# A transformer stack on one NeuronCore: register loops over the batches against a program that is written out

## The reference

```python
# L0
qh, kh, vh = q @ w_q, k @ w_k, v @ w_v            # 16 heads of 64
attn = einsum('bhqd,bhkd->bhqk', qh / sqrt(64), kh) + add_attn
attn = softmax(where(mask == 0, -1e9, attn))
out = layernorm(einsum('bhqk,bhkd->bhqd', attn, vh) @ w_o + residual)
# L1, twice: x with itself (masked), x with ctx_1024 (not masked), 16 heads of 32
x = layernorm(x + mha(x, memory))
# feed-forward
x = layernorm(x + relu(x @ w1 + b1) @ w2 + b2)
```

## Time and profile before

| | us |
|---|---|
| median of 3 runs | 4304.11 (4303.60 to 4305.34) |
| the profiled execution, as timed | 4310.14 |
| its span in the trace | 4308.4 |
| PE busy | 4168.9 (97%) |
| DVE busy | 3336.0 (77%) |
| ACT busy | 2840.6 (66%) |
| POOL busy | 1618.3 (38%) |

### The profile page before, as it was taken

How to read it: one execution, slowest core, us unless ns; L and a number is a source line. 1 busy time by engine, 2 the same in 40 slices (tenths; PEclk the granted TensorE clock), 3 DMA queues, 4 the chain that set the end, 5 groups by cost and what they waited for, 6 DMA issues and landing times. The chain is left out here.

```text
span 4308.4 us, 79964 instructions
## 1 busy us (share of the span) xinstructions
PE 4168.9 (97%) x23152; PEld 3401.2 (79%) x23152; DVE 3336.0 (77%) x6955; ACT 2840.6 (66%) x6169; POOL 1618.3 (38%) x1801
## 2 busy tenths in 40 slices
PE   7999999999999999999999999999999999999999
PEld 6888888888888777777777777777777767888887
DVE  6777778788888889889988999998899995333334
ACT  6666666666666678888888889888888883111111
POOL 2222222232333345555555546556555651110101
PEclk9999999999999999999999999999999999999999
DMA  2221112112111210000000021100101111100100
GB/s 94 66 64 51 61 51 81 49 62 69 51 61 51 77 59 21 26 31 30 31 15 31 23 72 47 40 25 32 35 30 37 54 57 64 40 29 34 49 29 35
DMA packets 108998, 200.82 MB, mean 47 GB/s; under 512 B 12208, under 2 KB 12208, under 8 KB 108720
## 3 DMA queue, kind: packets, MB, share of 16 engines
q1 hardware_dynamic: 108720, 197.73, 14.0%
HBM read 155.73 MB, written 41.94 MB: 46 GB/s over the span
## 5 line engine op out<-in xcount | busy, mean ns | idle before, releaser
L1672 POOL TENSOR_SCALAR QS<-QK 32x1024 fp32r<-32x1024 f32 (+2 forms) x1152 | 1164.8, 1011 | 1448.1 <-DVE QK L1351 626.5
L1174 ACT ACTIVATE R<-psT 128x512 fp32r<-128x512 f32 x1536 | 913.1, 594 | 453.8 <-PE psT L926 439.8
L1166 ACT ACTIVATE PR<-PR,MN 128x512 f32<-128x512 f32 x1536 | 1103.0, 718 | 56.0 <-DVE MN L1336 37.8
L1444 DVE TENSOR_TENSOR R<-psT,R 128x512 fp32r<-128x512 f32 x1536 | 1046.7, 682 | 27.2 <-issue 14.1
L926 PE MATMUL psT<-ID,PR 128*128 128x128 f32 x6144 | 928.6, 274 | 31.4 <-DVE R L1444 24.5
L926 PEld LDWEIGHTS psT<-ID,PR 128*128 128x128 f32 x6144 | 754.2, 141 | 258.6 <-issue 26.6
L1336 DVE CUSTOM_DVE_ANT_0 PR<-psS,RAW 128x512 f32<-128x512 f32 x1024 | 699.0, 683 | 284.0 <-PE psS L907 231.8
L948 PE MATMUL psV<-R 128*64 128x512 f32 (+1 forms) x3072 | 895.6, 400 | 11.7 <-DVE OG L1364 10.4
L948 PEld LDWEIGHTS psV<-R 128*64 128x64 f32 (+1 forms) x3072 | 457.0, 154 | 176.9 <-DVE R L1444 12.6
L910 PE MATMUL psS<-QS 128*128 128x512 f32 x1024 | 466.1, 455 | 28.1 <-DVE MN L1336 9.8
L1196 ACT ACTIVATE PR<-psS,COLS 128x512 f32<-128x512 f32 x128 | 88.3, 690 | 549.1 <-PE psS L866 549.1
(11 more groups left out here) (128 smaller groups left out, 8248.7 us busy)
## 6 DMA issues: line engine op xcount, KB each, us to landing
x<-Y SPq DMA_DIRECT2D x96, 256.0 KB, 2.1
RAW<-x SPq DMA_DIRECT2D x96, 256.0 KB, 2.7
Y<-x SPq DMA_DIRECT2D x96, 256.0 KB, 3.5
RAW<-in_ctx_t SPq DMA_DIRECT2D x92, 256.0 KB, 2.8
RAW<-in_w SPq DMA_DIRECT2D x68, 256.0 KB, 2.8
RAW<-in_x SPq DMA_DIRECT2D x60, 256.0 KB, 3.6
RAW<-in_side SPq DMA_DIRECT2D x60, 256.0 KB, 2.5
Y<-in_x SPq DMA_DIRECT2D x32, 256.0 KB, 4.2
```

What stands on the lines that cost most here:

```text
L1166: nc.scalar.activation(prob(st, k), prob(st, k), ACT.Exp, bias=MN[:, k % 8:k % 8 + 1], scale=-1.0, accum_out=row_sums(st, SM, g)[:, qt, j: ...
L1174: nc.scalar.activation(PT[h % 2][:, 0, :, qt * P:(qt + 1) * P], turned(place[st.name][k]).rearrange("p (k t) -> p k t", k=NT), ACT.Copy).t ...
L1444: nc.vector.tensor_tensor(lo, turned(place[st.name][k]).rearrange("p (k t) -> p k t", k=NT), f32(hi), ALU.subtract).then_inc(t_evac, 1)
L1672: nc.gpsimd.tensor_scalar(to, pair, 1.0, 1.0, ALU.mult, ALU.mult).then_inc(stacked, 1)
```

## The change

The five register loops are gone. `passes` and the programs of FF now call the middle batch six times in a Python loop, so each batch of each stage has its own instructions, every wait compares with a constant, and no engine branches. `turns`, `counts`, the lists of names and the three `gate` functions with all their calls are taken out; what a wait needs is now carried by the instruction itself or by a waiting instruction ahead of it. The computing instructions and their order on every engine are the same. The program of PE grows from 10,088 to 25,949 instructions, that of DVE from 3,521 to 7,055, of ACT from 2,527 to 5,073, of POOL from 1,615 to 2,448, of SP from 780 to 843.

```diff
@@ Tally @@
     def done(self, n):
-        v = self.unit * (n + 1) + self.credit
-        return v if self.turn is None else self.turn * (self.per * self.unit) + v
+        return self.unit * (n + 1) + self.credit
...
-@contextmanager
-def turns(eng, count, tallies):
-
-    first = [t.n for t, _ in tallies]
-    with eng.Fori(0, count) as r:
-        for t, per in tallies:
-            t.per, t.turn = per, r
-        yield r
...
@@ passes @@
-                with turns(eng, B - 2, [(tal[k], per[k]) for k in dict.fromkeys(own) if k in tal]) as r:
-                    run(middle_pass(i), r + 1)
+                for batch in range(1, B - 1):
+                    run(middle_pass(i), batch)
                 run(last_pass(i), B - 1)
...
@@ SP, the load of x @@
                 sp.wait_ge(x_hi, tal["x_hi"].done(n - 2))
-                gate()
                 sp.dma_start(xs[:, tal["xs"].slot(i)], dram[src][b, tt * P:(tt + 1) * P, :]).then_inc(
                     tal["xs"].sem_of(i), 16)
...
@@ PE, FF @@
-            with turns(pe, B - 2, [(tal["xs"], NT), (tal["j"], NT), (tal["u"], NF), (tal["h"], NF), (tal["acc"], NT)]):
+            for _ in range(B - 2):
                 ff()
...
```

More of the change, by code:

```diff
@@ L1 @@
-from contextlib import ExitStack, contextmanager
+from contextlib import ExitStack
 B, S, D, FF = 8, 512, 512, 2048
@@ L436, in __init__ @@
         self.sem, self.unit, self.credit = sem, unit, credit
-        self.n, self.per, self.turn, self.marks = 0, 0, None, {}
+        self.n, self.marks = 0, {}
     def next(self):
@@ L467, in done @@
     def done(self, n):
-        R = len(self.sems)
-        v = self.unit * (n // R + 1) + self.credit
-        return v if self.turn is None else self.turn * (self.per // R * self.unit) + v
-@contextmanager
-def turns(eng, count, tallies):
-    first = [t.n for t, _ in tallies]
-    with eng.Fori(0, count) as r:
-        for t, per in tallies:
-            t.per, t.turn = per, r
-        yield r
[L481 to L485, removed]
+        return self.unit * (n // len(self.sems) + 1) + self.credit
 def build(nc, x, ctx_t, side, key_mask, pair_mask, w, rows, cols, out):
@@ L623, in f32 @@
             return ap.bitcast(F32)
[L625 to L632, removed]
         def by_parts(st):
@@ L673, in projected, with passes @@
             return psJ[:, n % 2].rearrange("p (t h c) -> p t h c", t=2, c=st.dk)
-        def passes(eng, tal, names, run, settled):
+        def passes(run, settled):
             run(opening(), 0)
             for i, st in enumerate(STAGES):
[L679 to L684, removed]
                 run(first_pass(i), 0)
                 settled(st)
-                per["var"] = 2 * NT if by_parts(st) else NT
-                with turns(eng, B - 2, [(tal[k], per[k]) for k in dict.fromkeys(own) if k in tal]) as r:
-                    run(middle_pass(i), r + 1)
+                for batch in range(1, B - 1):
+                    run(middle_pass(i), batch)
                 run(last_pass(i), B - 1)
@@ L823, in settled @@
                     weight_gone(buffer)
-            passes(sp, tal, ["xs", "x_hi", "s", "y"], run, settled)
+            passes(run, settled)
             def ff_inputs(b):
@@ L839, in _ @@
             settled(None)
-            with turns(sp, B - 2, [(tal[k], NT) for k in ("xs", "x_hi", "y", "y_done")]) as r:
+            for r in range(B - 2):
                 ff_stores(r)
@@ L1065, in settled @@
                 need_weight(st.name, "O", KT - 1)
-            passes(pe, tal, ["xs", "s", "exp", "spread", "t", "pv", "o_lo", "j", "stack"], run, settled)
+            passes(run, settled)
             def ff():
@@ L1241, in run @@
                         relu(k)
-            passes(act, tal, ["t", "t_own", "s", "pv", "o_lo", "pv_evac", "j", "j_evac", "stack"], run, lambda st: None)
-            with turns(act, B - 2, [(tal["j"], NT), (tal["u"], NF), (tal["h"], NF)]):
+            passes(run, lambda st: None)
+            for _ in range(B - 2):
                 for f in range(NF):
@@ L1275, in _ @@
             dve.sem_inc(h_lo, 4)
-            def gate():
-                dve.sem_inc(gate_dve, 1)
             def x_lo_part(tt):
@@ L1532, in settled @@
                     dve.wait_ge(rows_full, rows_seen[0])
-            passes(dve, tal, ["x_hi", "s", "exp", "t_hi", "t", "pv_half", "pv_own", "o_hi", "j", "j_hi", "j_own", "y"], run, settled)
+            passes(run, settled)
             dve.wait_ge(rows_full, rows_seen[0] + 48)
@@ L1550, in batch @@
                     totals()
-            per = dict(x_hi=NT, j=NT, j_own=NT, h=NF, used=NF, hi=NF, res=NT, acc_own=NT, rstd=NT, y_sum=NT, mv=NT, gain=NT)
-            with turns(dve, B - 2, [(tal[k], per[k]) for k in per]):
+            for _ in range(B - 2):
                 batch(True)
@@ L1594, in _ @@
             pool.wait_ge(qs_zero, 1)
-            def gate():
-                pool.sem_inc(gate_pool, 1)
             def residual(tt):
@@ L1734, in settled @@
                     rows_of(st.rows)
-            passes(pool, tal, ["recip", "j", "s", "spread", "t", "pieces", "y"], run, settled)
-            with turns(pool, B - 2, [(tal[k], NT) for k in ("y", "mv", "var", "res", "rstd")]):
+            passes(run, settled)
+            for _ in range(B - 2):
                 for tt in range(NT):
```

11 lines of the change are left out of this document (removed).

## The result

| | before | after |
|---|---|---|
| median, us | 4303.85 (4302.62 to 4305.34, 4 runs) | 4265.73 (4264.71 to 4269.16, 4 runs) |
| the traced execution, as timed | 4310.14 | 4264.71 |

The ratio is 0.9913, 95% interval 0.9896 to 0.9930: 38.1 us less. I had forecast 27.3 less, 4277, and a range of 4265 to 4290. The result lies 0.7 us inside the lower end of that range.

A forecast was written before the change was run, and what follows sets the result against it. PE was taken as the bound, busy 4168.9 of 4308.4 us, so only its standing could shrink. Terms -22.8 - 6.5 - 1 + 0 + 3 = -27.3 took the median 4304.11 to 4277 us (chance 0.65), range 4265 to 4290.

The forecast's parts named there:

- Step 1: Branches back of SA's and CA's loops: removing them saves 14.94 us in SA and 7.87 in CA, -22.8 us.
- Step 2: POOL's gates ahead of its pieces: 15 stalls of PE's line 910 shorten by 0.43 us each, -6.5 us.
- Step 3: DVE's gates ahead of its reduction: dropping them starts it up to 0.19 us earlier, -1 us; SP's gates 0.
- Step 4: POOL's pieces beside DVE's line 1293 in L0: PE's 6.5 us of waits could go either way, taken as 0.
- Step 5: Extra instruction packets in L0 and FF meet loads of x: 3.2 hits at 1 us each, +3 us.
- Only the branches pay: Rival for POOL's gates: its own instruction costs what was put down to the gate; 4284 us, chance 0.25.
- straight code stalls as the branches did: Rival: each block of written-out code makes an engine wait once, so nothing is won; 4304 us, chance 0.04.
- only the branch itself is saved: Rival: 30 branches at PE's median 0.208 us save only 6.2 us; 4298 us, chance 0.02.
- The fetches collide: Rival: instruction packets hit x's load in all 18 middle batches of L0 and FF, +43 us; 4317 us, chance 0.04.

The follow-up runs named there:

- e3: Kernel before with only the middle batches of SA and CA written out, L0a, L0b and FF still loops, all gates kept: 4283.93 us, ratio 0.9950.
- e9: Kernel before with only SP's loops written out, the other four engines keeping their loops, all gates kept: 4300.31 us, ratio 0.9984.
- e5: Everything written out as in the changed kernel, but POOL's gates kept, those of DVE and SP gone: 4277.92 us, ratio 0.9932 to before.
- e6: Everything written out as in the changed kernel, but DVE's gates kept, those of POOL and SP gone: 4266.33 us, ratio 0.9904 to before.
- e1: Kernel before, unchanged, run again for a second trace: 4305.8 us, ratio 0.9999.
- e12: Kernel before with SA, CA and all first and last batches straight without gates; L0a, L0b and FF keep loops and gates: 4290.16 us, ratio 0.9959.
- e10: The changed kernel, unchanged, run again for a second trace: 4267.75 us, ratio 0.9908 to before.
- e11: The changed kernel with 32 counting instructions put ahead of PE's program: 4264.38 us, ratio 0.9902 to before.
- e7: Kernel before, loops and gates kept, with 128 counting instructions put ahead of PE's program: 4318.27 us, ratio 1.0025.
- e4: Kernel before with only L0a, L0b and FF written out, SA and CA still loops, all gates kept: 4316.48 us, ratio 1.0026.

## Why the prediction was right or wrong

My forecast had the largest cost right, and it was 10.8 us short of the 38.1 measured: it had no term for SP and for the loop's part of the stalls, and too small ones for POOL's gates elsewhere. The range held by 0.7 us. The runs give 22.6 us for the loops of SA and CA (e3), 6.7 for SP's loops (e9) and some 9 for POOL's gates (e5 against e6, less the late loads of x). That is 38; after has one late load of x, 3.2 us, which leaves 35 beside 38.1. The rest lies within the error: by the intervals e3 is good to 6 us either way and e9 to 4. What the register instructions of PE, DVE, ACT and POOL cost apart from this is in it unseparated.

- **Step 1, the branches, -22.8: right, and closer than it could know.** e3 measured 22.6, with an interval of 6 us to either side. Taking whole batches between like stalls, and not the idle times, catches costs that the step did not see: in the trace that it used three of SA's five batches had 3.4 us at half clock, some 5 of its 14.94 us, and how many have it changes from one execution to the next. The same sum over e1's trace, which has two, is 22.1. The step said that L0 gives nothing because its body is short. That held for before, and not as a rule: e12 has the same body at another place, at 3.2 to 4.4 us a branch. And L0's loops did cost SP's register instructions.
- **Step 2, POOL's gates, -6.5: the mechanism was right, the size too small.** The stall fell by 0.57 us in SA, 0.51 in CA and 0.35 at the starts of SA and CA, and not by 0.43. The gates' part is 0.35 of it each time, 5 us in all, so at these stalls I had priced them too high. The other 0.2 went with the loop and had no term. And "the other pieces give nothing" was wrong: the gates cost 0.55 us a batch of SA and CA, of which 0.35 are the stall, and 0.2 a batch of L0, 9 in all. The smaller places in SA and CA I didn't follow up.
- **Step 3, DVE's gates, -1: right within what can be measured.** They did delay each reduction, by 0.15 us (0.19 behind its matmul with them, 0.03 to 0.04 without, where I had expected 0.04 to 0.08), but e6 and after are the same within their intervals, as nobody waited.
- **Step 4, POOL beside DVE in L0, 0: wrong.** I had both ends and no row to choose by. PE's wait went from 6.5 to 2.5 us. e5 has 6.2 and e6 2.5, so it goes with POOL's gates. Of these 4 us L0's batches show 2.5 (93.55 in e5, 93.34 in e6), which is part of the 9 above.
- **Step 5, packets, +3: the sum was right by luck.** I had 3.2 hits at 1 us each. In after one batch was hit for 3.2 us, in e10 two for 3.5 together: fewer and dearer. The step had a packet's place in the load at random; what the runs show is that only those which start early in it count.
- **The missing step is SP.** I had looked only at SP's gates and called them free; the register instructions ahead of x's issue cost 0.3 us a batch of L0 and FF, 5.4 us by the batches and 6.7 by the times. The sign was in the earlier trace rows: the undisturbed batch there already waits 0.43 us for x. I read that row as the floor against which to price an accident. It was a wait on the path, which an earlier issue could remove.

*Only the branches pay* is refuted by e5 and e6, and by e3, which gains 22.6 of the 38.1; *straight code stalls as the branches did* and *only the branch itself is saved* are refuted by e3. *The fetches collide* happens, but in none (e11) to two (e10) of the eighteen batches.

## What to carry to other kernels

Before pricing the instructions that an engine's queue gives up, go through the waits that return in every batch, also those of 0.4 us, and ask of each whose instructions stand ahead of what ends it; the engine that issues the DMAs counts as much as one that computes. A loop of long bodies should be priced by whole batches with and without a branch, and the granted clock of each of these batches belongs beside its time. And any edit ahead of such a loop may change its price by more than the edit is worth, in either direction: compare the batches of loops that the edit didn't touch before you believe a total.

## What the runs showed of the hardware that I had not expected

- The cost of a branch back depends on where the body lies in its engine's program, and on chance. One body of SA cost 1.8 us (e7), 2.8 (e1) and 6.3 (e4) a branch, the last two with 1.4 and 5.5 us at half clock in it on average, and L0a's cost nothing in before and 3.2 to 4.4 in e12, where DVE's and POOL's loops lay 28 instructions earlier.
- One 16 KB packet of instructions that starts 1.3 to 2.1 us after a load of 256 KB was issued makes it 4.7 to 5.7 us long instead of 3.4 to 3.9, though the packet takes about 1 us of one of 16 DMA engines. One that starts 2.6 to 3.0 us after does nothing.
- An instruction that does nothing but count, ahead of a POOL piece, costs 0.11 us (0.19 between pieces with it, 0.08 without). Ahead of DVE's reduction it costs 0.15 us (0.19 after the matmul with it, 0.03 to 0.04 without), and the kernel nothing.
